# Second relation pass: the 16-relation table from two node blocks per product step, on the two row halves of TensorE

## The reference, cut to what matters

```
h = maximum(layernorm(x), 0)
for r in range(16):
    m = m + where(etypes == r, 1, 0)[:, None] * (h[src] @ weight[r])
x = x + segment_sum(m, dst)
```

## Time and profile before

| | us |
|---|---|
| Median of 3 runs | 8904.81 |
| Lowest and highest | 8902.08, 8905.78 |
| The profiled execution, its own time | 8892.44 |
| Its span in the profile | 8890.7 |
| TensorE busy (share of the span) | 5945.9 (67%) |
| GpSimd busy | 4978.1 (56%) |
| VectorE busy | 4692.0 (53%) |
| ScalarE busy | 1527.9 (17%) |
| Mean granted clock of TensorE | 0.643 |

### The profile page before, as it was taken

How to read it: one execution, slowest core, us unless ns; L and a number is a source line. 1 busy time by engine, 2 the same in 40 slices (tenths; PEclk the granted TensorE clock), 3 DMA queues, 4 the chain that set the end, 5 groups by cost and what they waited for, 6 DMA issues and landing times.

```text
span 8890.7 us, 135028 instructions
## 1 busy us (share of the span) xinstructions
PE 5945.9 (67%) x42197; PEld 4316.1 (49%) x42197; DVE 4692.0 (53%) x10280; ACT 1527.9 (17%) x4329; POOL 4978.1 (56%) x5265
## 2 busy tenths in 40 slices
PE   1277777777777877333333357777776878788777
PEld 1266666666666466333333322222225555555555
DVE  3499999999999299222222220000005555555555
ACT  1111111111112211000000000000003333333333
POOL 0376666666664176777777731111104777777776
PEclk9555655555555555555555579999995665656666
DMA  5555555555554354111111169999992222222222
GB/s 105 97 99 97 94 95 97 93 96 96 94 96 89 129 100 91 26 26 26 26 26 26 26 257 426 401 426 399 426 414 67 83 81 82 81 81 82 82 82 69
DMA packets 803225, 1176.34 MB, mean 132 GB/s; under 512 B 623063, under 2 KB 656279, under 8 KB 775466
## 3 DMA queue, kind: packets, MB, share of 16 engines
q1 hardware_dynamic: 630458, 923.60, 32.8%
q0 software_dynamic: 172528, 250.20, 13.4%
HBM read 921.76 MB, written 258.23 MB: 133 GB/s over the span
## 4 chain that ended last, share of the span: by engine, by line
POOL 28%; issue 21%; DVE 20%; DMA 14%; PE 11%; DVEq 3%; SPq 1%; ACT 0%; POOLq 0%; ACTq 0%
POOL arena L478 28%; DMA arena<-B_d 11%; DVE ps L1199 6%; DVE arena L1200 5%; PE ps L898 5%; DVE arena L1202 4%; DVE pair L1175 3%; PE ps L800 2%; PE ps L843 2%; DVEq L1167 1%; PE ps L829 1%; DMA attr_s<-arena 1%; PE ps L793 1%; DVEq L1168 1%; DMA arena<-tab,idx 1%
## 5 line engine op out<-in xcount | busy, mean ns | idle before, releaser
L478 POOL DMA_INDIRECT arena<-tab,idx x4992 | 4730.1, 948 | 2252.4 <-issue 1606.7
L843 PE MATMUL ps<-arena 128*128 128x64 f32 x6656 | 1399.0, 398 | 1067.2 <-DMA arena<-tab,idx 1065.0
L829 PE MATMUL ps<-arena 128*64 128x98 f32 x15872 | 1457.3, 359 | 686.9 <-DVE arena L1202 686.1
L843 PEld LDWEIGHTS ps<-arena 128*128 128x128 f32 x6656 | 1337.6, 307 | 1137.8 <-issue 1065.1
L829 PEld LDWEIGHTS ps<-arena 128*64 128x64 f32 x15872 | 1180.8, 211 | 929.6 <-DVE arena L1202 801.1
L898 PE MATMUL ps<-arena,ev 128*64 128x512 f32 (+1 forms) x4836 | 1113.0, 606 | 365.4 <-DMA arena<-B_d 291.4
L1200 DVE TENSOR_TENSOR arena<-arena,ps 128x784 f32<-128x784 f32 x992 | 954.9, 963 | 0.0
L898 PEld LDWEIGHTS ps<-arena,ev 128*64 128x64 f32 x4836 | 383.2, 144 | 1094.9 <-issue 750.2
L1161 DVE TENSOR_TENSOR arena<-relT,ps 128x1024 f32<-128x1024 f32 x624 | 759.5, 1217 | 251.9 <-issue 245.0
L515 POOL DMA_INDIRECT ev<-emb_d,dvI x186 | 175.3, 943 | 1257.8 <-PE ps L898 1043.7
L1175 DVE TENSOR_TENSOR X<-X,ps 128x64 f32 x832 | 183.8, 221 | 1169.2 <-PE ps L843 1154.6
(11 more groups left out here) (211 smaller groups left out, 3909.9 us busy)
## 6 DMA issues: line engine op xcount, KB each, us to landing
arena<-B_d SPq DMA_DIRECT2D x186, 3136.0 KB, 17.2
B_d<-stg SPq DMA_DIRECT2D x248, 784.0 KB
arena<-tab,idx POOLq DMA_INDIRECT x4992
arena<-rel_d SPq DMA_DIRECT2D x208, 256.0 KB
tab<-arena SPq DMA_DIRECT2D x26, 1024.0 KB, 3.9
attr_s<-arena SPq DMA_DIRECT2D x13, 512.0 KB, 8.8
stg<-attr_s SPq DMA_DIRECT2D x208, 32.0 KB
rec_d<-arena SPq DMA_DIRECT2D x6, 832.0 KB, 24.6
```

The lines of the kernel that those rows point to most:

```text
L478: pool.indirect_dma_start(gat[:, r, k * width:(k + 1) * width], None, table, bass.IndirectOffsetOnAxis(ap=idx[:, r, k:k + 1], axis=0)).the ...
L829: ins = pe.matmul(ps[3 + j % 2][a * KP:(a + 1) * KP, i2 * KC:(i2 + 1) * KC], Lw[:, j % 2, t, :], Rc[:, j % 2, t, :], start=True, stop=True)
L843: ins = pe.matmul(ps[6 + r % 2][:, k * D:(k + 1) * D], S[:, r % 2, k, :], gat[:, r, k * D:(k + 1) * D], start=True, stop=True)
```

## The change

Each product step handles two blocks. `HS` is packed to 64 numbers per block, so that one transpose turns two blocks at once: the even block's features come out on rows 0 to 63, the odd one's on rows 64 to 127. `HT` gets 128 rows, and `WR` is loaded twice, once to each half of the rows, so a second DMA stands at L314. A pair's products are issued for columns 0 to 511 of both blocks and then for columns 512 to 1023 of both, the even block's on the lower 64 rows of the array and the odd block's on the upper 64. The banks stay as they were (2 and 3 even, 4 and 5 odd) but are handed on by column halves: new semaphores `half_ps` and `half_mv` cover the first 512 columns of a pair, `proj_ps` and `proj_mv` the second. Projections 0 and 2 keep their form.

```diff
-        HT = sb("HT", [DA, 2, BG * P])
+        HT = sb("HT", [P, 2, BG * P])
-        WR = sb("WR", [D, NREL * D])
+        WR = sb("WR", [2 * D, NREL * D])
...
-            sp.dma_start(WR[:].rearrange("i (r o) -> i r o", r=NREL), rel_w.rearrange("r i o -> i r o")).then_inc(s_["rel_in"], 16)
+            for t in range(2):
+                sp.dma_start(WR[t * D:(t + 1) * D, :].rearrange("i (r o) -> i r o", r=NREL), rel_w.rearrange("r i o -> i r o")).then_inc(s_["rel_in"], 16)
...
# ScalarE
+                    if n == 1:
+                        act.copy(HS[:, q, 0:BG * D].rearrange("p (b f) -> p b f", b=BG), Hv[:, bass.ds(j * BG, BG), :]).then_inc(s_["hs_ok"], 1)
...
+                    if n == 1:
+                        act.copy(HT[:, q, 0:BG * D], ps[q][:, 0:BG * D]).then_inc(s_["ht_ok"], 1)
...
-                        for b in (2 * u, 2 * u + 1):
-                            if not has_nodes(j, b):
-                                continue
-                            act.wait_ge(s_["proj_ps"], (n * NJ + j) * BG + b + 1)
-                            for w in range(2):
+                        pair_of = [b for b in (2 * u, 2 * u + 1) if has_nodes(j, b)]
+                        if not pair_of:
+                            return
+                        for w in range(2):
+                            if w == 0:
+                                act.wait_ge(s_["half_ps"], j * 2 + (u + 1))
+                            else:
+                                act.wait_ge(s_["proj_ps"], (n * NJ + j) * BG + 2 * u + 2)
+                            for b in pair_of:
                                 ins = act.copy(TO[:, b * NREL * D + w * 512:b * NREL * D + (w + 1) * 512], ps[2 + 2 * (b % 2) + w][:])
-                            ins.then_inc(s_["proj_mv"], blocks_done(j, b))
+                            if w == 0:
+                                ins.then_inc(s_["half_mv"], 1)
+                        ins.then_inc(s_["proj_mv"], sum(blocks_done(j, b) for b in pair_of))
...
# TensorE
-                    for b in range(BG):
-                        ins = pe.transpose(ps[q][0:DA, b * P:(b + 1) * P], HS[:, q, b * DA:(b + 1) * DA], ident[:])
+                    for b in range(BG if n != 1 else BG // 2):
+                        if n == 1:
+                            ins = pe.transpose(ps[q][:, b * P:(b + 1) * P], HS[:, q, b * P:(b + 1) * P], ident[:])
...
+                    if n == 1:
+                        for u in range(BG // 2):
+                            pair_of = [b for b in (2 * u, 2 * u + 1) if has_nodes(j, b)]
+                            if not pair_of:
+                                continue
+                            for w0 in range(0, width, 512):
+                                if w0 == 0:
+                                    wait(pe, s_["half_mv"], j * 2 + u)
+                                else:
+                                    pe.wait_ge(s_["proj_mv"], (n * NJ + j) * BG + 2 * u)
+                                for b in pair_of:
+                                    t = b % 2
+                                    ins = pe.matmul(ps[2 + 2 * t + w0 // 512][:], HT[t * D:(t + 1) * D, q, u * P:(u + 1) * P],
+                                                    w[t * D:(t + 1) * D, w0:w0 + 512], start=True, stop=True)
+                                    if w0 + 512 >= width:
+                                        ins.then_inc(s_["proj_ps"], blocks_done(j, b))
+                                if w0 == 0:
+                                    ins.then_inc(s_["half_ps"], 1)
+                        return
...
-            pe.wait_ge(s_["rel_in"], 16)
+            pe.wait_ge(s_["rel_in"], 32)
```

More of the change, by code:

```diff
@@ L226, in gnn_kernel @@
             stair_out tiles_ok blk_in stair_done dve stair_d x_in ln_var ln_std ln_ok hs_ok hT_ps ht_ok proj_ps
-            proj_mv nrm_in nrm_out idx_ok pc_ok rec2_out beg_oh beg_ps off_in off_ps tile_in tile_ps iota_ok
+            half_ps half_mv proj_mv nrm_in nrm_out idx_ok pc_ok rec2_out beg_oh beg_ps off_in off_ps tile_in tile_ps iota_ok
             tix_ok row_d wm_ok recT cols_ok ohp_ok lhs_ok bmm bev l1_done emb_ok emb_out hop_mm sum_ok ev_a ev_d
@@ L554, in stage @@
                     wait(act, s_["hT_ps"], n * NJ + j - 1)
-                    act.copy(HS[:, q, :], H[:, bass.ds(j * (BG * DA), BG * DA)]).then_inc(s_["hs_ok"], 1)
+                    if n == 1:
+                        act.copy(HS[:, q, 0:BG * D].rearrange("p (b f) -> p b f", b=BG), Hv[:, bass.ds(j * BG, BG), :]).then_inc(s_["hs_ok"], 1)
+                    else:
+                        act.copy(HS[:, q, :], H[:, bass.ds(j * (BG * DA), BG * DA)]).then_inc(s_["hs_ok"], 1)
                 def stationary(j, q):
@@ L560, in stationary @@
                     wait(act, s_["proj_ps"], (n * NJ + j - 1) * BG)
-                    act.copy(HT[:, q, :], ps[q][0:DA, :]).then_inc(s_["ht_ok"], 1)
+                    if n == 1:
+                        act.copy(HT[:, q, 0:BG * D], ps[q][:, 0:BG * D]).then_inc(s_["ht_ok"], 1)
+                    else:
+                        act.copy(HT[0:DA, q, :], ps[q][0:DA, :]).then_inc(s_["ht_ok"], 1)
                 def move_pair(j, u):
@@ L780, in turn @@
                     wait(pe, s_["ht_ok"], n * NJ + j - 1)
-                    for b in range(BG):
-                        ins = pe.transpose(ps[q][0:DA, b * P:(b + 1) * P], HS[:, q, b * DA:(b + 1) * DA], ident[:])
+                    for b in range(BG if n != 1 else BG // 2):
+                        if n == 1:
+                            ins = pe.transpose(ps[q][:, b * P:(b + 1) * P], HS[:, q, b * P:(b + 1) * P], ident[:])
+                        else:
+                            ins = pe.transpose(ps[q][0:DA, b * P:(b + 1) * P], HS[:, q, b * DA:(b + 1) * DA], ident[:])
                     ins.then_inc(s_["hT_ps"], 1)
@@ L793, in products @@
                             ins = pe.matmul(ps[bank][:, c0:c0 + width], HT[0:k, q, b * P:(b + 1) * P], w[0:k, :], start=True, stop=True)
[L794 to L802, removed]
+                            ins.then_inc(s_["proj_ps"], 1)
                 turn(0, 0)
```

## The result

The kernel after takes 8817.24 us, the median of four runs (8814.56 to 8820.72), against 8903.44 before (8898.19 to 8905.78, now four runs): a ratio of the runs of 0.9904, 95% interval 0.9887 to 0.9921. Forecast were 8819. Run again in two later comparisons it gave 0.9898 (0.9883 to 0.9913) and 0.9900 (0.9884 to 0.9917).

What follows compares the result with a forecast made beforehand. TensorE was taken to bound the stage that makes the table. 86.7 us gained there, less 0.7 for the second load of WR, off the median: 8904.8 - 86.0 = 8818.8, so 8819 us; range 8806 to 8850.

Steps and rivals of the forecast that it cites:

- Product steps: Table's stage: two products on the two row halves run together, 1.71 + 0.04 us a step at the present clock.
- Rival (3): Table's stage: row halves take turns, so only transposes are saved: 8900 us; chance 0.09.
- Rival (2): Products in order, the odd block's first instruction after the even block's second: 58 us gained, 8847 us; chance 0.13.
- rival (4): Row halves take turns and each weight load, 0.33 us, is no longer hidden: slower, 8964 us; chance 0.04.
- The banks: Table's stage: banks of one column half come round in 3.45 us a pair at the present clock, 0.04 of it wait.
- The clock: Table's stage: TensorE's granted clock rises from 0.50 to 1.00 from about the second group after the restart.
- The stores: Table's stage at the higher clock: stores freeing half the table's buffer set the pace, 6.4 us a group.
- The start: VectorE's normalisation waits 0.34 us instead of 2.43 for ScalarE's square root: 2.1 us gained.
- The second load: Preparation, SP queue: loading WR a second time costs 0.7 us, bounds 0 and 4.6.
- The sum: Table's stage gains 86.7 us, 86.0 with the second load; other passes 0; 8819 us in all; chance 0.45.

Runs made afterwards that it cites:

- the one with the late load: The kernel after with the second load of WR moved from the preparation to behind the loads of Web, where the first pass begins: 8808.37 us, ratio 0.99.

## Why the prediction was right

By its own steps:

- **Product steps.** Both row halves run together: loads in twos 0.85 us apart, as read from the column halves of the hops. Rival (3), halves in turns, is refuted, and its price when forced is above the kernel before.
- **No offset.** Rival (2), for which the Trainium skill's page TensorE: Matmul & The Clock Gate, section "The mechanism", was named, did not come: the odd block's first load stands with the even block's first. The hops' rows decided rightly over that reading of the section. (The 3.07 times that the prediction takes from it stands one section further on in that page of the Trainium skill, "Measured speedup vs the span model", and is for four row tiles, which no run here has.) Bare weight loads, rival (4), did not come either.
- **The banks.** At 0.50 a pair was forecast at 3.45 us and took 2878.95 - 2875.64 = 3.31. The forecast chain was 0.14 long, 0.10 of it in the step from the end of the copies to the next load, 0.06 us instead of 0.16.
- **The clock.** Forecast 1.00 from about the second group after the restart; it rose within the first group of all and, after the idle stretch, again in the first group after the restart. That it would fall again was not in the forecast. Around 2917 us it cost little: that group took 7.8 us and the next 4.9. In the last block it cost more: its end came 2.3 us after its first copy began, where 1.4 was forecast. Two other profiles (the second of the kernel after, and the one with the late load) have no fall before the last copy, and their stages took 117.5 us, against 119.2 and 119.3 in the two that have it. What the Trainium skill says in the same page, section "What's actually happening", of a busy TensorE does not agree with the profiles: busy for 150.00 of 150 us it had 0.50, busy for 34.22 of 46 it had 1.00.
- **The stores.** Next late were the stores, as forecast, at 6.27 us a group (forecast 6.4): four copies 2.05 for 2.14, the rest 4.21 for 4.25. The sum from the restart to the last copy was 68.9 us, and it took 2974.2 - 2906.2 = 68.0.
- **The start.** VectorE's wait for the square root fell from 2.43 to 0.36 us: 2.07 of the 2.1 forecast.
- **The second load.** Forecast 0.7 us; its issues show 1.3, the medians nothing.
- **The sum.** Stage 86.7 forecast, 87.7 measured from the first two profiles and up to 89.4 from the later ones of after. The passes behind gave nothing back (5834.8 and 5833.8 us).

The profiles alone would have shown 75.5 us: the first profile of after had a preparation 11.7 us longer than that of before, while the runs of before in the same comparison lay 6 to 13 us above its profile. The forecast was taken off the median and not off that profile, and so did not carry this difference. The agreement of 8819 with 8817.24 to 2 us owes something to luck: in the two later comparisons the change was worth 89.6 and 88.8 us (8896.09 to 8806.48, 8890.33 to 8801.56), against 86 forecast.

## What to carry to other kernels

A product of 64 contraction rows uses half the array. Placing a second independent one on the other 64 rows, with banks of its own, ran it for free, and with both halves in use together TensorE was also granted its full clock, so the stage's TensorE time fell to a third. The clock is not kept for certain: here it fell back twice after waits. Look then for what the faster engine collides with: here every 6.27 us a buffer half waited for a 1 MB store, which could be summed from the profile before as four copies, one landing time and some 0.35 us of signals and issue. Sending the store in two parts gained another 6.8 us, and then the rate of the DMA engines was the limit. When a stage that was not edited moves between two profiles, profile the same kernel again before explaining it.

## What the runs showed of the hardware

- In this stage the clock went with the use of both halves together, not with TensorE's busy time and not with the packing: 0.50 with one half busy all the time, 0.50 with the halves in turns at 135.25 of 140 us, 1.00 with both together at 34.22 of 46 us. With both together it was still 0.50 at first and twice later, the second time after 1.77 us of idleness (at 2970.47 us). In the second profile of after it stayed at 1.00 through an idle time of the same length (at 2904.15 us).
- The time from the end of streaming to ScalarE's first copy was 0.47 us at 0.50 and about 0.30 at 1.00; a sum for the higher clock should not take it over from the lower.
- 1 MB stores kept their landing time at more than twice the rate: median 3.9 us before, at 140 GB/s, and 3.9 after, when the stretch from 2920 to 2966 us moved 327 GB/s. Stores of 512 KB took 4.1 us each at 378 GB/s, with the DMA engines at a share of 1.02.
- Two profiles of the same kernel had the first gather at 375.2 and 360.6 us; ten profiles of the later comparisons had it between 358.7 and 363.3.
